# A window-ratio kernel on one core: 32 duos of boxes kept ahead instead of 30, a warm-up of TensorE, statistics moved inside a duo, duo 0 cut into pairs

## The reference

```python
g = groupnorm(x, 32 groups of 6 channels, eps=1e-5)   # mean and variance over rows, W and the group's channels
s = box_sum(g, axis W, 5)                             # zero padded
num = box_sum(s * s, channels, 20)
d = box_sum(box_sum(g * g, axis W, 5), channels, 20)
c1 = box_sum(ones(128), 5)                            # 5 inside, 3 or 4 at the edges
out = x + nan_to_num(num / (d * c1[None, None, :, None]), nan=1.0)
```

## Time and profile before

| | |
|---|---|
| median of 3 runs | 364.64 us (364.48 to 364.65) |
| the profiled execution | 364.6 us, span 362.6 us |
| PE busy | 345.5 us, 95% of the span |
| DVE, ACT, POOL busy | 316.9, 272.1, 267.6 us |
| bytes moved | 62.63 MB, mean 173 GB/s |
| mean granted clock of PE | 0.997 |

### The profile page before, as it was taken

The page is one execution under the profiler, slowest core; times in us unless marked ns, Lnnn a source line. Parts: engine busy times, 40 slices in busy tenths (PEclk is TensorE's granted clock), DMA queues, the critical chain, the costliest instruction groups (busy, mean ns, idle before and its releaser), DMA issues.

```text
span 362.6 us, 7725 instructions
## 1 busy us (share of the span) xinstructions
PE 345.5 (95%) x2810; PEld 335.1 (92%) x2810; DVE 316.9 (87%) x662; ACT 272.1 (75%) x407; POOL 267.6 (74%) x216
## 2 busy tenths in 40 slices
PE   3999989999999999999989999999999999999991
PEld 3999989999999999999988999999999999999981
DVE  1999984666799999999997999999999999999984
ACT  1556559989999998899946777777778777777761
POOL 5000036687888888878848899999999999999833
PEclk9999999999999999999999999999999999999998
DMA  8999500379999985222222054777677776777679
GB/s 239 327 328 327 172 2 0 89 233 279 286 287 284 284 262 178 89 87 89 87 89 72 17 134 87 175 176 173 163 164 164 165 163 154 157 156 160 165 172 274
DMA packets 70837, 62.63 MB, mean 173 GB/s; under 512 B 1424, under 2 KB 66960, under 8 KB 70800
## 3 DMA queue, kind: packets, MB, share of 16 engines
q1 hardware_dynamic: 66480, 50.34, 44.7%
q0 software_dynamic: 4320, 11.80, 18.3%
HBM read 25.17 MB, written 25.17 MB: 139 GB/s over the span
## 4 chain that ended last, share of the span: by engine, by line
PE 72%; ACT 5%; DVE 5%; issue 2%; POOL 1%; POOLq 0%; DVEq 0%; ACTq 0%
PE N L680 23%; PE U L671 16%; PE S L671 12%; PE D L680 12%; PE D L736 5%; PE S L680 5%; ACT xs L586 2%; DVE late_triples L833 1%; ACT xc L550 1%; ACT q L604 1%; DVE ratio L957 1%; ACT u L567 1%; POOL xs L459 1%; POOL xc L451 1%; DVE N L962 0%
## 5 line engine op out<-in xcount | busy, mean ns | idle before, releaser
L451 POOL TENSOR_TENSOR xc<-xs,mean_c 128x768 f32<-128x768 f32 x32 | 58.6, 1832 | 47.6 <-DVE mean_c L846 45.0
L671 PE MATMUL S<-b,xs 128*128 128x128 f32 x564 | 72.4, 279 | 5.8 <-DMA xs<-x 5.8
L467 POOL TENSOR_TENSOR xs<-xs,ratio 128x768 f32<-128x768 f32 x32 | 58.4, 1825 | 25.0 <-DVE ratio L968 25.0
L671 PEld LDWEIGHTS S<-b,xs 128*128 128x128 f32 x564 | 68.8, 196 | 5.9 <-issue 5.8
L451 POOL TENSOR_TENSOR xs<-xs,mean_c 128x768 f32<-128x768 f32 x31 | 64.6, 2083 | 0.0
L962 DVE SCALAR_TENSOR_TENSOR N<-N,q 128x768 f32<-128x768 f32 x62 | 59.3, 957 | 1.9 <-PE N L680 1.8
L604 ACT ACTIVATE q<-D 128x768 f32<-128x768 f32 x48 | 38.9, 811 | 23.2 <-PE D L736 13.7
L610 ACT ACTIVATE q<-q 128x768 f32<-128x768 f32 x62 | 52.3, 844 | 2.0
L680 PE MATMUL N<-b_r,xs 128*128 128x138 f32 (+2 forms) x384 | 52.2, 285 | 0.1
L680 PE MATMUL N<-b,xs 128*128 128x138 f32 x372 | 50.0, 283 | 0.0
L680 PEld LDWEIGHTS N<-b_r,xs 128*128 128x128 f32 x384 | 48.4, 190 | 0.5 <-issue 0.3
(11 more groups left out here) (115 smaller groups left out, 627.0 us busy)
## 6 DMA issues: line engine op xcount, KB each, us to landing
out<-xs SPq DMA_DIRECT2D x31, 768.0 KB, 5.0
xs<-x SPq DMA_DIRECT2D x18, 768.0 KB, 5.2
xs<-xs POOLq DMA_DIRECT2D x30, 384.0 KB, 4.1
xs<-x SPq DMA_DIRECT2D x7, 1536.0 KB, 15.2
out<-xs SPq DMA_DIRECT2D x1, 384.0 KB, 5.3
out<-xs SPq DMA_DIRECT2D x2, 192.0 KB, 4.1
```

Of the source, the lines that this page charges most:

```text
L451: nc.gpsimd.tensor_tensor(pairs(xc_of(n)), pairs(x_flat(n)), mean, ALU.subtract)\
L467: nc.gpsimd.tensor_tensor(x_flat(n), x_flat(n), ratio_of(n), ALU.add)\
L671: mm = nc.tensor.matmul(bank[:, i, chunk], rows[:, at:at + 128], weights[:, :], start=True, stop=True)
```

## The change

- RAW_DUOS becomes 32 (`RAW` stays 15, with the new `KEPT_DUOS` = 30), so duos 30 and 31 get `box_raw` as well and `box_s` runs for batch 1 only. Their boxes are first kept in `q`, stored by SP to DRAM during the start of batch 0, and loaded back behind the store of step 10 into the slot of step 8, which is free then. DVE mends their edges ahead of duo 27. ACT's `take_root` of duos 0 and 1, which write `q`, wait for those two stores. SWAPPED moves from 28 to 30 with it, FIRST_FILL from 28 to 30.
- DVE first sets a constant, and PE multiplies it with itself 10 times ahead of all else.
- The block means are averaged in 4 matmuls of 128 columns (two loads each, behind duos 11, 19, 26 and at the end) in place of 8 of 192.
- In a duo with statistics, the first comes between t2 and the ratio, the others behind the ratio as before; every fourth duo has one more. A set's first wait is now ahead of its first duo's `quotient`. None is left for duo 28's larger share.
- Duo 0 is centred and squared by pairs, as duo 32 is already, and DVE copies U of duo 0 instead of ACT.
- `box_u(32)` waits for the product of the deviations (`dev_used`) only, not for the sums of squares.
- `scale_c` takes the place of `ssq_c`, so a wait for a store goes; the last pair is stored from ACT's queue.

```diff
-RAW = 15
-RAW_DUOS = RAW * STEP_DUOS
+RAW = STEPS - 1
+RAW_DUOS = STEPS * STEP_DUOS
+KEPT_DUOS = RAW * STEP_DUOS
+
+WARM_UPS = 10
...
+AVERAGED_BEHIND = (11, 19, 26)
...
-SET_DUO, SET_LATE_DUO = (5, 5, 3), (5, 5, 6)
+SET_DUO, SET_MORE, SET_LATE_DUO = (5, 5, 3), 4, (5, 5, 5)
...
+            for i in range(STEP_DUOS):
+                sp.wait_ge(raw_kept, KEPT_DUOS + i + 1)
+                sp.dma_start(spilled_boxes[:, i * DCOLS:(i + 1) * DCOLS], first_raw_box(KEPT_DUOS + i))\
+                  .then_inc(spilled[i], 16)
...
                 store(t)
+                if t == MORE_SLOT - RAW + 2:
+                    sp.wait_ge(stored[t % 2], 16 * (t // 2))
+                    for i in range(STEP_DUOS):
+                        sp.wait_ge(spilled[i], 16)
+                    sp.dma_start(raw_box(KEPT_DUOS, STEP_DUOS), spilled_boxes).then_inc(reloaded, 16)
...
-                if n == DUOS:
+                if n % DUOS == 0:
                     for i in range(DUO):
                         nc.gpsimd.tensor_tensor(pairs(xc_of(n))[:, i, :], pairs(x_flat(n))[:, i, :], mean[:, i, :],
                                                 ALU.subtract).then_inc((first_xc_ready, xc_ready)[i], 1)
...
                 act.wait_ge(d_ready, n + 1)
+                if n < STEP_DUOS:
+                    act.wait_ge(spilled[n], 16)
...
             square_xc(1)
-            keep_u(0)
             act.wait_ge(inv_ready, 1)
...
+            store_last_pair(act, 1, last_stored)
...
                 if n == MEAN_AT + BOX_AHEAD + 1:
-                    pe.wait_ge(ssq_ready, 2)
+                    pe.wait_ge(dev_used, 1)
...
+            def average_blocks(k):
+
+                pe.wait_ge(block_measured, 2 * k + 2)
+                return nc.tensor.matmul(means_ps, averager[0][:, :], triples[0][:, :, 4 * k:4 * k + 4, 1],
+                                        start=k == 0, stop=k == LOADS // 2 - 1)
...
+            pe.wait_ge(warm_up_ready, 1)
+            for _ in range(WARM_UPS):
+                nc.tensor.matmul(U[:, 0, 0:W], warm_up, warm_up, start=True, stop=True)
...
                 if before_ratio:
                     before_ratio()
+                for j, g in arrived[:1]:
+                    measure(1, j, g)
                 dve.wait_ge(t1_ready, n + 1)
                 dve.wait_ge(t2_ready, n + 1)
                 nc.vector.scalar_tensor_tensor(t1, t1, 2.0, in_bank(N), ALU.add, ALU.mult).then_inc(ratio_ready, 1)
+                for j, g in arrived[1:]:
+                    measure(1, j, g)
...
+            nc.vector.memset(warm_up, 1.0).then_inc(warm_up_ready, 1)
...
             keep_offsets()
+            keep_first_u(0)
...
             fold_variance(0).then_inc(inv_ready, 1)
             mend_edges(0, STEP_DUOS)
-            dve.wait_ge(u_ready, 2)
-            nc.vector.tensor_copy(pairs(u[:, 1, :]), in_bank(U)).then_inc(us_ready, 1)
-            dve.wait_ge(raw_kept, RAW_DUOS)
-            mend_edges(STEP_DUOS, RAW_DUOS - STEP_DUOS)
+            keep_first_u(1)
+            mend_edges(STEP_DUOS, KEPT_DUOS - STEP_DUOS)
...
             for n in range(TOTAL - TAIL):
+                if n == KEPT_DUOS - BOX_AHEAD - 1:
+                    dve.wait_ge(reloaded, 16)
+                    mend_edges(KEPT_DUOS, STEP_DUOS)
...
+                    more = n < SWAPPED and n % SET_MORE == 0
+                    arrived = arrived[:(SET_DUO if n < SWAPPED else SET_LATE_DUO)[j] + more]
+                    unmeasured = unmeasured[len(arrived):]
+                quotient(n, arrived, behind_t1=spread_late if n == MEAN_AT else None,
+                         before_ratio=scale_late_bands if n == VAR_AT else None)
```

More of the change, by code:

```diff
@@ L176, in window_ratio_kernel @@
         raw_kept = sem("raw_kept")
+        spilled = [sem(f"spilled{i}") for i in range(STEP_DUOS)]
+        reloaded = sem("reloaded")
         edges_ready = sem("edges_ready")
@@ L339, in wait_loaded1, with store_last_pair @@
             eng.wait_ge(loaded1[j], 16 * 2 * (LATE_SETS[j][1] - LATE_SETS[j][0]))
+        def store_last_pair(eng, i, done):
+            first = ROWS - DROWS + i * PAIR
+            eng.wait_ge(tail_ready[i], 1)
+            eng.dma_start(out[BATCH - 1, first:first + PAIR, :, :].rearrange("h w c -> w h c"),
+                          x_rows(LAST)[:, i * PAIR:(i + 1) * PAIR, :]).then_inc(done, 16)
         @block.sync
@@ L386, in _ @@
             sp.dma_start(dram_rows(out, LAST - 1), x_rows(LAST - 1)).then_inc(stored[1], 16)
[L387 to L392, removed]
+            store_last_pair(sp, 0, stored[0])
+            sp.wait_ge(stored[0], 16 * (BATCH * STEPS // 2 + 1))
+            sp.wait_ge(last_stored, 16)
             sp.wait_ge(stored[1], 16 * (BATCH * STEPS // 2))
@@ L530, in keep_raw @@
                 act.wait_ge(raw_in_psum, n + 1)
-                nc.scalar.activation(pairs(raw_box(n)), in_bank(raw_bank(n)), ACT.Copy).then_inc(raw_kept, 1)
+                nc.scalar.activation(pairs(first_raw_box(n)), in_bank(raw_bank(n)), ACT.Copy).then_inc(raw_kept, 1)
             def square_xc(n):
-                if n == DUOS:
-                    act.wait_ge(first_xc_ready, 1)
-                    act.wait_ge(u_ready, n - LATE_RING + 1)
+                if n % DUOS == 0:
+                    act.wait_ge(first_xc_ready, batch(n) + 1)
+                    if n:
+                        act.wait_ge(n_ready, (XC2_SLOT + LATE_SLOTS) * STEP_DUOS)
                     nc.scalar.activation(pairs(xc2_of(n))[:, 0, :], pairs(xc_of(n))[:, 0, :], ACT.Square)\
@@ L708, in box_u @@
             def box_u(n):
-                if n == DUOS:
-                    pe.wait_ge(first_xc2_ready, 1)
+                if n % DUOS == 0:
+                    pe.wait_ge(first_xc2_ready, batch(n) + 1)
                 else:
@@ L788, in _ @@
                 box_raw(n)
-                if n % LOAD_DUOS == LOAD_DUOS - 1 and n > LOAD_DUOS:
-                    average_block(n // LOAD_DUOS - 1)
-            for j in range(FIRST_FILL // LOAD_DUOS - 1, LOADS):
-                mm = average_block(j)
+                if n in AVERAGED_BEHIND:
+                    average_blocks(AVERAGED_BEHIND.index(n))
+            for k in range(len(AVERAGED_BEHIND), LOADS // 2):
+                mm = average_blocks(k)
             mm.then_inc(mean_in_psum, 1)
@@ L862, in spread_late @@
                 squares = nc.vector.tensor_tensor(late_dev[:, :, :], late_dev[:, :, :], dev[1], ALU.mult)
+                squares.then_inc(dev_used, 1)
                 sum_m2(1)
-                own[0] += 1
-                squares.then_inc(dve_own, 1)
-                dve.wait_ge(dve_own, own[0])
+                dve.wait_ge(dev_used, 1)
                 sum_squares(1, late_dev[:, :, :])
@@ L935, in mend_edges @@
                 half = len(EDGES) // 2
+                of_edges = offsets_ps if n < KEPT_DUOS else offsets
                 for first, w in ((1, 0), (1 + half, W - half)):
                     edge = boxes[:, :, :, w:w + half]
-                    add = offsets_ps[:, :, first:first + half].unsqueeze(1).to_broadcast([128, duos * DUO, CHUNKS, half])
+                    add = of_edges[:, :, first:first + half].unsqueeze(1).to_broadcast([128, duos * DUO, CHUNKS, half])
                     ins = nc.vector.tensor_tensor(edge, edge, add, ALU.add)
```

49 lines of the change are left out of this document (26 added, 23 removed).

## The result

| | before | after |
|---|---|---|
| median | 364.57 us (364.44 to 364.87, 22 runs) | 365.52 us (364.11 to 368.64, 22 runs) |
| ratio, 95% interval | | 1.0033 (1.0022 to 1.0043) |
| the profiled execution, its span | 364.6, 362.6 us | 366.26, 364.0 us |
| mean granted clock of PE | 0.997 | 0.994 |

The changed kernel is slower by 0.95 us, where 363.5 was forecast, and 365.52 lies outside the range of 362.2 to 364.9. Its executions also spread over 4.5 us, those of before over 0.4.

A forecast was written before the change was run, and what follows sets the result against it. PE was taken as the bound, working 345.5 of 362.6 us. The terms 0 - 0.4 + 0.8 - 1.4 - 0.1 = -1.1 on 364.6 gave 363.5 us, range 362.2 to 364.9.

The forecast's parts named there:

- The mend: Ahead of duo 27: mending two reloaded duos, 2 x 0.16 us, falls into DVE's wait for ACT, so 0.
- The set wait: Ahead of duo 7 instead of behind it: last load landed at about 92.3, so 0, at worst 0.5 us.
- The early statistic: Raw duos, between t2 and ratio: delays the ratio 0.27 or 0.08 us; +0.8 in all, bounds 0 and 3.5.
- rival A: Raw duos: early statistic costs nothing, ACT's idle time takes it up; -1.9, 362.5 us; chance 0.2.
- my count of one stall in four duos: Raw duos: PE's N is held up once in four duos, 2 x 0.27 plus 3.3 x 0.08 us.
- Rival C: Duos 7 to 28: every duo pays for the statistic between t2 and ratio; +3.5, 366.2 us; chance 0.12.
- Between the batches: Late mean: five statistics instead of eight behind ratio 28; PE's saved 2.68 us turns idle; -1.4, bounds -2.0 and -0.8.
- The start: Start of batch 0: centring by pairs and DVE's copy of U bring the scaling forward; -0.4, bounds -0.6 and 0.
- The load: Load of batch 0: two more boxes offset by averaging and warm-up; mean moves under 0.1; 0, bounds -0.1 and +0.4.
- rival B: Load phase becomes PE's, mean up to 0.4 later, start's gain eaten; 363.9 to 364.2 us; chance 0.17.
- The end: Last pair on ACT's queue goes out some 0.4 us sooner, but bytes decide; -0.1, bounds -0.5 and +0.2.
- rival D: Between the batches: PE's clock falls while it stands for 1.2, 1.4 and 0.8 us; 366.5 us; chance 0.04.

The follow-up runs named there:

- experiment 1: Changed kernel with the late mend moved behind the ratio of duo 26, operands unchanged: 364.00 us, ratio 0.9993.
- experiment 2: Changed kernel with the late mend's offsets kept in PSUM, the mend between t2 and ratio of duo 26, that duo's statistic behind the ratio: 364.87 us, 1.0005.
- experiment 12: Kernel before plus unused 6-column DVE additions in duos 38 to 57, second input in PSUM or SBUF: 364.91 us, one execution.
- experiment 7: Changed kernel with late mend and set waits moved behind the ratio, and no statistic ahead of any ratio: 363.72 us, 0.9980.
- experiment 3: Changed kernel with the late mend from PSUM ahead of ratio 26 and all statistics behind the ratio, set waits still ahead: 364.77 us, 1.0005.
- experiment 5: Changed kernel with the late mend behind ratio 26, and set waits with their duo's first statistic behind the ratio: 363.71 us, 0.9978.
- experiment 4: Kernel before with only the new counts of statistics per duo, still 30 raw duos: 363.53 us, 0.9974.
- experiment 9: Changed kernel with late mend and set waits moved behind the ratio, and the last pair stored from SP's queue: 363.46 us, 0.9971.
- experiment 6: Changed kernel with only the set waits moved behind the ratio, mend left in place: 364.35 us, 1.0003.
- experiment 8: Changed kernel with late mend and set waits moved behind the ratio, without the ten warm-up products: 363.51 us, 0.9972.

## Why the prediction was wrong

- **The mend: 0 forecast, 2.4 us in the profile, 0.6 to 1.5 in the medians.** This is the step that failed. "Mending two duos (2 x 0.16 us) falls into DVE's wait for ACT: 0" took its price from the early mend of the same form. But the row's inputs are `xs,N`, and the changed code reads `offsets` from SBUF for the late one. In every DVE row with two tensors in the earlier trace rows one of them is N, S or D, in PSUM. A form whose operands change place is an operation that the trace before does not show, and had to be bounded from both sides; the upper bound would have been two of POOL's instructions, 2 x 1.8. Experiments 1, 2 and 12 show the mechanism. The Trainium skill (SBUF — State Buffer, Who interferes with whom) states the rule: a VectorE instruction with two SBUF inputs and a GpSimd instruction reading SBUF share one read interface, and the later waits for the whole of the other. The traces agree, with the ends 0.02 to 0.05 us apart. It speaks against this change, and I did not weigh it.
- **The set wait: "0, at worst 0.5".** It took one set's landing time against one duo. Duo 11's set lands when DVE stands ahead of t1: 0.33 us in the changed kernel's profile, 0.75 and 0.61 in those of experiments 1 and 2, 0.3 (mend moved) to 1.2 (not moved) in the medians. Behind the ratio, where it stood before the change, it had DVE's statistics alone behind it; ahead of t1 it has t1, the ratio and PE's N.
- **The early statistic: +0.8 forecast, 0.0 measured** (experiment 7; 0.1 in 3). The term came out as rival A had it, and my count of one stall in four duos was wrong. That the same statistic taken out from behind the ratio leaves the next t1 early by as much would explain it, but no run separates this from ACT's idle time. The sign I named, 8.6 us for two duos in place of 8.46, could not tell: the kernel before takes 8.46 to 8.82 between duos 20 and 28. Rival C, the way listed to a slower kernel, did not occur; it got slower by the two faults above, of which no rival spoke.
- **Between the batches: -1.4 forecast, -1.10 measured** (-1.10 in experiment 5, -0.89 and -0.91 with six statistics in 4 and 7), within its bounds. The five statistics are there (2.40 for 3.77 us), less the 0.27 us that the one ahead of ratio 28 delays it. That PE's two boxes turn into idle time was right (experiments 4 and 7), as long as DVE is the bound.
- **The start: -0.4 forecast, -0.35 to -0.41 measured.** Centring by pairs and DVE's copy did what was worked out: the first scaling came at 56.47 where 56.43 was forecast, U at 67.95 where it had been 68.30. Neither store of `q` held up a root; they landed in 2.3 us, not the 4 to 5 of the forecast.
- **The load: 0 forecast, the mean 0.15 later**, within -0.1 to +0.4, on the side of rival B: DVE stood 0.95 us until ACT had kept the 30th box, at 50.20 where 50.0 was forecast (before the change it waits for the 28th). The warm-up does as it says: 1.58 for 2.90 us; it spares 0.57 here in a profile and nothing in the medians.
- **The end: -0.1 forecast, +0.2 measured**, and up to +0.8 once the loop is earlier. ACT's queue is at most a small part of it; the store behind the accumulating DMA is suspected.
- **The clock (rival D)** did not fall in the profiled execution: it stood at 1.00 from 5.0 to 359.96 us, and the last matmul ended at 356.13. The mean of 0.994 against 0.997 comes from the stretch behind that. It came up 7.0 us sooner, not 4.7.

In the profile the terms add up: -0.35 for the start, +0.28 up to duo 26, +2.45 for the mend, -1.10 at the join and +0.2 at the end make, but for rounding, the +1.4 of the span. Without its two faults the change comes to 363.71, close to the 363.5 of the sum, but that is partly luck, since the misses cancel: 0.8 less for the statistics against 0.3 less at the join and up to 0.9 more at the end. The counts alone do no worse (363.53).

**Open.** Why single executions spread by more than 1 us even without the faults (experiment 5: 363.18 to 364.58, against 363.43 to 363.62 for nine of ten in experiment 4), and what binds the end. The 32 raw duos by themselves do not make the spread: experiments 7 and 9 have them, too, and nine of eleven lie within 363.54 to 363.82, six of seven within 363.33 to 363.54. An accumulating DMA issued sooner was not tried.

## What to carry to other kernels

Price an instruction by a row with the same operands in the same memories: here a small DVE addition with both inputs in SBUF cost what was left of POOL's running instruction, so keep one input in PSUM or place it where POOL waits for DVE. Move a wait for a load only where little is queued behind it on an in-order engine. Where two engines meet at a join, first even out the statistics (one line, -1.0 us) and only then spare PE work, which gave nothing here while six statistics stood on DVE.

## What was unexpected of the hardware

- The hold-up is by whole instructions and repeats: the first of two 24-column mends ended about with POOL's L500 (178.21), the second was held again, to the end of L484 (179.99), which followed at once. DVE did not get in between: 2.88 us for 0.28 us of work. Who begins first seems to decide: the probe at 330.07, 0.04 us behind POOL's start, was held for 0.99 us, while one that began with POOL's instruction (320.42 both) took 0.17.
- A profiled execution need not show the usual price (an inference from the times, as above): in experiment 6 the row holds 2.6 us more, but ten of twelve executions lie only 0.4 to 1.0 us above the median of experiment 5.
- Ten dummy products bring PE's granted clock up 7.0 us sooner (5.0 against 11.9 us), and the median of the kernel does not move (experiment 8). The moment varies from execution to execution: 4.2 to 7.1 us in the nine profiles with the products, 9.2 to 11.9 in the five without.
